# Layers: the turn, scale and split of the normalised unit in the first half step of the next unit, and its last addition one half step later

## The reference, cut to what matters

```python
def _layer(x, wqkv, qs, ksc, wo, lg, lb, w1, b1, w2, b2):
    h = shift_token(x)                      # half of the channels from the token before
    q, k, v = split(h @ wqkv)               # 8 heads of 64
    q, k = rotary_xpos(l2norm(q) * qs, l2norm(k) * ksc)
    o = local_attention(q, k, v)            # window 128, looks one window back
    x = x + o @ wo
    h = shift_token(x)
    h = (h - mean) / sqrt(var + 1e-05) * lg + lb
    a, g = split(h @ w1 + b1)               # 2 x 682
    return x + (a * gelu(g)) @ w2 + b2
```

## Time and profile before

| | us |
|---|---|
| median of three runs | 4161.38 |
| the profiled execution's own time | 4156.13 |
| its span | 4154.3 |
| PE busy in the span | 3759.8 (91%) |
| DVE busy | 3079.0 (74%) |
| ACT busy | 2612.0 (63%) |
| POOL busy | 1887.2 (45%) |

### The profile page before, as it was taken

How to read it: one execution, slowest core, us unless ns; L and a number is a source line. 1 busy time by engine, 2 the same in 40 slices (tenths; PEclk the granted TensorE clock), 3 DMA queues, 4 the chain that set the end, 5 groups by cost and what they waited for, 6 DMA issues and landing times.

```text
span 4154.3 us, 88049 instructions
## 1 busy us (share of the span) xinstructions
PE 3759.8 (91%) x33070; PEld 2895.4 (70%) x33070; DVE 3079.0 (74%) x7229; ACT 2612.0 (63%) x5759; POOL 1887.2 (45%) x1444
## 2 busy tenths in 40 slices
PE   4799999999998759999999999989999999999997
PEld 2354545445544347888888888878888888888886
DVE  4677777777776358777787877777888788788884
ACT  1355555555555447777777777767777777767774
POOL 1212322232233035555555555555666565656664
PEclk7799999999999879999999999999999999999999
DMA  4444244353441120000000000011000000000000
GB/s 124 88 74 119 58 112 102 73 125 75 92 128 34 33 67 31 15 20 18 17 20 15 20 17 18 17 43 41 22 28 27 23 26 22 26 24 25 24 23 21
DMA packets 146019, 195.93 MB, mean 47 GB/s; under 512 B 21596, under 2 KB 119608, under 8 KB 145600
## 3 DMA queue, kind: packets, MB, share of 16 engines
q1 hardware_dynamic: 145600, 190.31, 18.4%
HBM read 113.66 MB, written 67.16 MB: 44 GB/s over the span
## 4 chain that ended last, share of the span: by engine, by line
PE 24%; DVE 14%; ACT 12%; DMA 8%; issue 5%; POOL 0%; DVEq 0%; SPq 0%; POOLq 0%; ACTq 0%
PE b_bank_m L1914 10%; DMA b_hs<-b_fr 8%; PE b_bank_p L1914 5%; ACT b_e L1794 4%; DVE b_e L2142 3%; PE b_bank_et L1979 2%; PE b_bank_t L1914 2%; DVE b_qk_rot L2111 2%; ACT L1837 2%; DVE b_rot L2115 2%; PE b_bank_ot L1994 2%; PE b_bank_s L1968 1%; ACT b_e_t L1804 1%; DVE b_ag L2206 1%; ACT b_ag L1829 1%
## 5 line engine op out<-in xcount | busy, mean ns | idle before, releaser
L728 ACT ACTIVATE a_e_t<-a_ring 128x1024 f32<-128x1024 f32 (+3 forms) x768 | 610.9, 809 | 528.5 <-PE a_ring L869 371.7
L1050 DVE TENSOR_REDUCE a_mx<-a_ring 128x2 f32<-128x1024 f32 (+3 forms) x768 | 724.5, 956 | 233.8 <-PE a_ring L869 113.1
L1682 POOL TENSOR_TENSOR b_e<-b_e,b_share 128x512 f32<-128x512 f32 (+1 forms) x512 | 505.9, 991 | 801.2 <-DVE b_share L2150 801.1
L1794 ACT ACTIVATE b_e<-b_e,b_bias 128x256 f32<-128x256 f32 (+1 forms) x1024 | 494.2, 486 | 164.7 <-DVE b_bias L2142 163.8
L2142 DVE CUSTOM_DVE_ANT_0 b_e<-b_bank_s,b_mask,b_inv 128x256 f32<-128x256 f32 (+1 forms) x1024 | 415.8, 460 | 31.1 <-PE b_bank_s L1968 31.1
L1667 POOL TENSOR_TENSOR b_qk_rot<-b_qk_rot,b_rot 128x512 f32<-128x512 f32 x256 | 351.7, 1384 | 130.1 <-DVE b_rot L2115 130.1
L1804 ACT ACTIVATE b_e_t<-b_bank_et 128x512 f32<-128x512 f32 (+1 forms) x512 | 287.2, 561 | 184.2 <-PE b_bank_et L1979 184.1
L882 PE MATMUL a_ring<-a_k_st,a_q_st 48*128 48x512 f32 (+3 forms) x1536 | 328.2, 424 | 77.4 <-ACT a_e_t L728 41.6
L907 PE MATMUL a_ring<-a_q_st,a_k_st 50*128 50x512 f32 (+3 forms) x1536 | 340.0, 441 | 40.7 <-ACT a_e_t L728 13.7
L907 PEld LDWEIGHTS a_ring<-a_q_st,a_k_st 50*128 50x128 f32 x1536 | 147.5, 189 | 298.0 <-issue 145.0
L1979 PE MATMUL b_bank_et<-b_ident,b_e 128*128 128x128 f32 x1920 | 310.8, 282 | 43.1 <-ACT b_e_t L1804 43.1
(11 more groups left out here) (238 smaller groups left out, 11010.3 us busy)
## 6 DMA issues: line engine op xcount, KB each, us to landing
a_q_st<-a_parts_q SPq DMA_DIRECT2D x192, 128.0 KB, 4.8
a_k_st<-a_parts_k SPq DMA_DIRECT2D x192, 128.0 KB, 7.5
a_parts_q<-a_qk_p SPq DMA_DIRECT2D x16, 1024.0 KB, 8.0
a_parts_k<-a_qk_p SPq DMA_DIRECT2D x16, 1024.0 KB, 8.1
b_fl<-f_rows SPq DMA_DIRECT2D x64, 256.0 KB, 4.1
a_xl<-in_L_attn_x SPq DMA_DIRECT2D x9, 1024.0 KB, 5.3
a_x<-in_L_attn_x SPq DMA_DIRECT2D x8, 1024.0 KB, 9.3
x_rows<-a_x SPq DMA_DIRECT2D x8, 1024.0 KB, 4.6
```

What stands on the lines that cost most here:

```text
L728: act.activation(e_t[:, step % 2, 2 * pair:2 * pair + 2, 0:cols], slot[:, :].rearrange("p (h t) -> p h t", h=2)[:, :, 0:cols], ACT.Exp).th ...
L1050: dve.reduce_max(mx[:, g % 2, :, pair, piece, t:t + 1], slot[:, :].rearrange("p (r c) -> p r c", r=2)[:, :, 0:cols], AX.X)\
L1682: pool.tensor_tensor(weights, weights, share[:, h % SPS, 2 * j:2 * j + 2].unsqueeze(2) .broadcast_to([P, 2, 2 * WIN - lo]), ALU.mult).then ...
L1794: ins = act.activation(weights, weights, ACT.Exp, scale=-1.0, bias=bias[:, h % SPS, at:at + 1], accum_out=total[:, h % SPS, at:at + 1])
```

## The change

The normalised unit's turn, scaling and split go to the first half step (NORM_AT 8), early in it on every engine; its last addition (ADD_AT 12) goes from the fourth half step to the first one that follows it, ahead of `row_tops`. The loads of the next layer's norm vectors stay where they were.

```diff
-MOMENTS_AT, NORM_AT, AG_AT, W2_AT, ADD_AT = 6, 7, 8, 10, 11
+MOMENTS_AT, NORM_AT, AG_AT, W2_AT, ADD_AT = 6, 8, 8, 10, 12
@@ next_layer (SP)
-                    if at == NORM_AT - 2:
+                    if at == AG_AT - 3:
@@ GpSimd
             for g in frame.range:
+                u = frame.unit(g, NORM_AT)
+                if u is not None:
+                    unit_lo(u)
                 if frame.half(g) is not None:
                     for j in range(PPS):
                         share_out(g, j)
-                u = frame.unit(g, NORM_AT)
-                if u is not None:
-                    unit_lo(u)
@@ ScalarE
                 if before is not None and g % SPW:
                     take_turned(before, 0)
+                u = frame.unit(g, NORM_AT)
+                if u is not None:
+                    unit_hi(u)
                 w = frame.window(g, OUT_AT)
...
                     square(w)
-                u = frame.unit(g, NORM_AT)
-                if u is not None:
-                    unit_hi(u)
@@ VectorE
                 if out is not None:
                     add_attention(out)
+                u = frame.unit(g, NORM_AT)
+                if u is not None:
+                    scale_unit(u)
                 turn = frame.window(g - 1, ROTATE_AT)
...
                     sum_squares(w)
-                u = frame.unit(g, NORM_AT)
-                if u is not None:
-                    scale_unit(u)
```

## The result

The changed kernel takes 4300.97 us (median of four runs, 4295.87 to 4326.47) against 4155.94 for the kernel before on the same chip (4145.05 to 4162.23): ratio 1.0364, 95% interval 1.0316 to 1.0412. It is slower by some 145 us. The forecast was 4340, with a range of 4256 to 4425. The profiled execution's span is 4297.9 us, 143.6 more than before.

A forecast was written before the change was run, and what follows sets the result against it. PE was taken as nearly full (96% busy), waiting on other engines' chain. A new serial chain costs 2.5 us over 62 units, 155 us, plus 26 for the clock: 181 on 4156.13 gives 4337, stated as 4340, range 4256 to 4425.

The forecast's parts named there:

- T: Start of `row_tops` in the fourth half step, the point from which the prediction measures all times.
- F: Start of `first_products` on PE; 10.27 us after T in unit 44 before the change, 11.15 in unit 43.
- The gain in the fourth half step: `add_unit` leaves the front of `row_tops`, shortening the chain by 0.60 us a unit; PE then waits for the `et` copy.
- The rotation, 4.14 by the second half step's row: DVE's four fourth-half-step rotation products slow from 3.26 to 4.14 us, as `add_turned` on POOL can now run beside them.
- T': The new T, start of the fourth half step's `row_tops` after `add_unit` has left its front.
- F at T' + 14.4: New serial chain before `first_products`, from rotation through `add_unit`, `row_tops`, `add_attention`, `scale_unit`, `unit_hi` and `unit_lo`, ends 14.4 us after T'.
- PE ready at 11.6 and 12.5: PE's own list before `first_products` done 11.6 us after T', 12.5 with row transposes; stalls 2.8 and 1.9 us.
- Taken back behind F, 1.1 and 0.2 us: After F, GELU's relatively sooner start returns 1.1 us in units with the 0.89 us stall, 0.2 in the others.
- Sum for a unit: Mean net cost over four kinds of unit, 2.5 us longer; over 62 units +155 us, before the clock.
- the rival without stretch: Fourth-half-step rotation keeps its 3.26 us, a unit costs 1.6 us, the clock stays: 4256 us; chance 0.14.
- The clock, 26 us: PE's clock falls after the longer stall before `first_products`, 1.7 us lost each, in half of 31 units: 26 us.
- At nothing: Delayed POOL, ACT and SP work such as `share_out`, `scale_k`, `finish` and the store stays covered, costing nothing.

The follow-up runs named there:

- the run with both shortenings: Changed kernel with scale_unit and unit_hi ahead of row_tops and the exponentials, first half step, and fourth-half-step q addition behind both rotation products: 4194.88 us, ratio 1.0100.

## Why the prediction was right

The mechanism was the one named: a chain of single instructions from T to F in place of PE's own work. Point by point:

- *The gain in the fourth half step, 0.60 us.* Measured 0.57 (20.67 to 20.10), and the wait for `et` was the one that came late next.
- *The rotation, 4.14 by the second half step's row.* Measured 4.23 in nearly every unit. The experiment with the addition behind both products shows the cause and the price: 1.07 us of rotation, some 66 us of time (against the 3.34 of the kernel before, the change itself added 0.9 us of it).
- *`row_tops` of the first half step at T' + 8.81.* Measured 8.83.
- *F at T' + 14.4.* Measured 13.83 (13.30 with a narrow mask). One term was mis-sized: `unit_lo`, taken at the 1.80 us of the earlier trace rows, takes 1.27. In the kernel before it ran beside the fourth rotation product and was itself stretched. I had seen that contention from DVE's side, and not carried it over to POOL's row.
- *PE ready at 11.6 and 12.5.* In unit 44 the stall begins at T + 11.94; `turn_unit` starts at 9.04, not 8.81, since it waits for `add_unit`'s end. Together with the earlier F, the stall is 1.88 us where I had 2.8, and 1.00 where I had 1.9. So PE's wait for `h_lo` is 87.2 us in total, below the 140 to 180 that I had named.
- *Taken back behind F, 1.1 and 0.2 us.* The 0.89 us stall is gone, as said. But these two came to 0.43 us a unit on the mean, and measured, without the clock, it is 0.27 (units 1 to 60): the first layer's units gave back only 0.14.
- *Sum for a unit.* Forecast 2.5 us without the clock; measured 2.33 with it. Some 0.15 of that is the clock: seven of the units 1 to 61 have first products of 10.2 to 10.3 us instead of 8.75. That leaves 2.18, so the sum was high by 0.3 us, 20 us in all. Here two misses partly cancel, which is luck: `unit_lo` alone would have made the sum 0.5 us too high, and what was taken back behind F made it 0.2 too low. (The 2.9 for the narrow mask should be 2.8 by its own terms, and the rival without stretch 4255; neither matters.)
- *The clock, 26 us.* Measured 7 x 1.5 = 11 us. I had half of the units with the longer stall, and 7 of the 16 units that have the stall of 1.9 us do have a fall; but there are 16 such units, not 31, since the narrow mask shortens the stall to 1.34 us in the others. What failed is the bound that I read from the earlier trace rows (no fall after 2.60 us, a fall after 2.88): here the clock falls behind stalls of 1.88 us. Windows around unit 52 (PE busy first, PEclk third last), whose first products begin at 3816.28:

```profile
3812.00:3816.00 4.00, 2.40 (x16) 1.85 (x14) 3.97 (x12) 2.64 (x10) 1.15 (x2) 1.00 0.03 7
3816.00:3820.00 4.00, 3.72 (x20) 3.73 (x21) 1.77 (x5) 3.12 (x7) 3.62 (x5) 0.62 0.03 9
3820.00:3824.00 4.00, 4.00 (x34) 4.00 (x34) 1.56 (x3) 1.93 (x4) 0.89 (x1) 0.95 0.00 0
```

- *At nothing: `share_out`, `scale_k`, `finish`, the stores.* Right. POOL's waits don't appear among PE's beyond what they were. That `finish` costs nothing holds only where the change puts it: ahead of `unit_lo` it costs 0.3 to 0.8 us a unit and more falls of the clock.

What stays open: of the 3.6 points, 2.6 are shown to lie in the order on the chain. The last one, 0.5 us a unit, is what is left when `turn_unit` itself stands in the first half step. The trace of the run with both shortenings says what holds it there: not `add_unit` but `turn_unit`'s place in PE's list, with `h_lo` behind it in half of the units and the row transposes in the rest. That is read from the rows; no run takes it away. Why the clock falls in some units and not in others with the same stall wasn't settled either (in the run with the addition for q behind both products it falls in 10 of the 16 units with a stall of 1.8 to 1.9 us).

## What to carry to other kernels

Before moving a serial hand-over between engines next to its consumer, add it up from the last thing that every engine in it must do first, and compare that with the consumer's own list: here 13.8 against 11.9 us. A wait that is long for its engine may be what keeps that engine from disturbing another, and taking it away has its price there. And taking a short instruction from ahead of the row that everybody waits for moved the wait twice here, first to `key_lo` and then to the sum of q: both times the next stretch took back 0.5 of the 0.6 us. It is worth following each reader behind it before counting the gain.

## What was not expected of the hardware

- In these traces GpSimd and VectorE held each other up by the whole instruction, and by turns. A share of 1.04 us that started behind the start of the first of four back-to-back rotation products took 3.21 us, and the four then took 2.47 us instead of 3.34. An addition of 1.25 us that got in between the third and the fourth took 1.65 us and made the fourth 1.75 us instead of 0.68. `row_tops`, which reads PSUM, kept its 0.47 us an instruction beside `unit_lo`.
- Which of the two is held up hangs on little. In unit 44 of the kernel before, `unit_lo` starts 0.02 us behind the fourth product (3370.01, 0.68 us) and takes 1.80 us. In unit 32 of the same kernel it starts 0.05 us ahead of it, and the product pays (DVE, then POOL):

```profile
2883.18 1.79 DVE L2115 TENSOR_TENSOR b_rot<-b_qk,b_tab 128x512 f32<-128x512 f32 x1
2883.14 1.29 POOL L1687 TENSOR_TENSOR b_h_t_lo<-b_ag,b_h_t_hi 128x512 fp32r<-128x512 f32 x1 [1.02 <-ACT b_h_t_hi L1822]
```

- `unit_lo` took 1.26 to 1.27 us in all 64 units of the changed kernel; its median before was 1.80 us.
- TensorE's clock fell to 1.2 GHz behind stalls of 1.88 us in the changed kernel, and stayed up behind one of 2.60 us in the kernel before. One fall costs 1.5 us when matmuls follow.
